# Feed-forward weight terms in six parts: three per head added by accumulating DMAs, three by GpSimd

## What is computed

```
xn = _layernorm(x)
x  = x + attention(xn) + ffn(xn)
attention: q,k,v = split(xn @ qkv_w + qkv_b); 16 heads of 128
           scores = q @ k.T + alibi (causal); softmax; ctx = attn @ v; ctx @ out_w + out_b
ffn:       gate = xn @ lut[gate_idx].T;  up = xn @ lut[up_idx].T
           h = silu(gate) * up;          out = h @ lut[down_idx].T
lut: 16 values; gate_idx, up_idx: 688x256; down_idx: 256x688
```

## Time and profile before

| | |
|---|---|
| median of 3 runs | 542.9 us (542.81 to 543.8) |
| the profiled execution | 543.26 us |
| its span in the trace | 541.5 us |
| busy | PE 493.8 us, DVE 414.2 us, POOL 403.6 us, ACT 360.9 us |

### The profile page before, as it was taken

The page is one execution under the profiler, slowest core; times in us unless marked ns, Lnnn a source line. Parts: engine busy times, 40 slices in busy tenths (PEclk is TensorE's granted clock), DMA queues, the critical chain, the costliest instruction groups (busy, mean ns, idle before and its releaser), DMA issues.

```text
span 541.5 us, 9700 instructions
## 1 busy us (share of the span) xinstructions
PE 493.8 (91%) x2826; PEld 422.4 (78%) x2826; DVE 414.2 (76%) x1067; ACT 360.9 (67%) x657; POOL 403.6 (75%) x312
## 2 busy tenths in 40 slices
PE   7896797999889988998899989997999989789998
PEld 6785576898779876987689768986798779578897
DVE  6796988788888878888788987888788886543541
ACT  3575867687767867595959685877678766824430
POOL 5533989788978998798969897889789979921400
PEclk9997999999999999999999999999999999979999
DMA  8204243332514070606160524134331514000001
GB/s 285 87 0 101 62 98 103 73 91 53 146 44 116 13 186 4 156 0 161 38 144 16 119 80 113 47 79 120 70 90 43 119 38 104 0 1 2 0 21 58
DMA packets 18948, 41.65 MB, mean 77 GB/s; under 512 B 4848, under 2 KB 7024, under 8 KB 18800
## 3 DMA queue, kind: packets, MB, share of 16 engines
q1 hardware_dynamic: 18928, 41.40, 30.2%
HBM read 11.83 MB, written 1.05 MB: 24 GB/s over the span
## 4 chain that ended last, share of the span: by engine, by line
POOL 44%; PE 23%; issue 21%; DVE 7%; ACT 3%; DMA 1%; POOLq 0%; DVEq 0%; ACTq 0%
POOL p_t_lo L1125 17%; POOL w_ffn L1153 15%; POOL work L1118 5%; PE ps_u L447 5%; PE ps_u L449 4%; PE ps_u L448 4%; DVE term L958 3%; PE ps_s L447 2%; PE ps_s L448 2%; PE ps_s L449 2%; POOL v_w_lo L1102 2%; POOL pad L1117 2%; POOL qk_w_lo L1097 2%; ACT ctx_t_hi L721 1%; DVE ctx_t_lo L898 1%
## 5 line engine op out<-in xcount | busy, mean ns | idle before, releaser
L1153 POOL TENSOR_TENSOR w_ffn<-w_ffn,term 128x1088 f32<-128x1088 f32 x60 | 155.0, 2584 | 45.4 <-DVE term L958 45.4
L1125 POOL TENSOR_TENSOR p_t_lo<-p_t_lo,p_t_hi 128x1024 fp32r<-128x1024 f32 (+2 forms) x60 | 133.1, 2251 | 0.0
L738 ACT ACTIVATE work<-work,neg_max 128x128 f32<-128x128 f32 (+7 forms) x128 | 99.0, 773 | 24.1 <-DVE neg_max L937 22.1
L937 DVE CUSTOM_DVE_ANT_0 work<-ps_s,alibi 128x128 f32<-128x128 f32 (+7 forms) x128 | 95.8, 749 | 0.0
L447 PE MATMUL ps_u<-p_t_hi,v_hi 128*128 128x512 f32 x192 | 70.5, 367 | 17.7 <-POOL p_t_lo L1125 17.4
L975 DVE STREAM_TRANSPOSE blocks<-work 128x512 f32<-128x512 f32 x120 | 65.3, 582 | 11.6 <-ACT work L750 11.6
L447 PE MATMUL ps_s<-k_hi,q_hi 128*128 128x256 f32 (+2 forms) x192 | 67.3, 350 | 5.3 <-DVE neg_max L937 5.3
L958 DVE TENSOR_SCALAR term<-codes,entry,table 128x1088 f32<-128x1088 uint8 x60 | 65.8, 1096 | 4.3 <-POOL w_ffn L1153 4.3
L449 PE MATMUL ps_u<-p_t_hi,v_lo 128*128 128x512 f32 x192 | 67.2, 350 | 0.0
L448 PE MATMUL ps_u<-p_t_lo,v_hi 128*128 128x512 f32 x192 | 67.0, 349 | 0.0
L448 PE MATMUL ps_s<-k_lo,q_hi 128*128 128x256 f32 (+2 forms) x192 | 65.8, 343 | 0.0
(11 more groups left out here) (148 smaller groups left out, 1271.1 us busy)
## 6 DMA issues: line engine op xcount, KB each, us to landing
p_t_lo<-blocks SPq DMA_DIRECT2D x240, 116.0 KB, 2.3
qk_raw<-w_qk SPq DMA_DIRECT2D x16, 256.0 KB, 2.7
w_ffn<-idx SPq DMA_DIRECT2D x1, 2176.0 KB, 11.0
v_raw<-w_v SPq DMA_DIRECT2D x8, 256.0 KB, 3.5
o_raw<-w_o SPq DMA_DIRECT2D x8, 256.0 KB, 2.9
out<-acc SPq DMA_DIRECT2D x8, 128.0 KB, 1.7
acc<-x SPq DMA_DIRECT2D x2, 256.0 KB, 3.0
acc<-x SPq DMA_DIRECT2D x1, 512.0 KB, 5.0
```

The lines of the kernel that those rows point to most:

```text
L738: act.activation(slot(i), slot(i), ACT.Exp, bias=neg_max[:, col:col + 1], scale=-1.0, accum_out=row_sum[:, col:col + 1]).then_inc(exp_done, 1)
L937: dve.tensor_tensor_reduce(slot(i).rearrange("p (b c) -> p b c", b=banks), made_of, alibi[:, p, S - width:S].rearrange("p (b c) -> p b c", ...
L1125: pool.tensor_tensor(rows, rows.bitcast(F32), chunk_rows(0, chunk).bitcast(F32), ALU.subtract).then_inc(upper_lo, 1)
L1153: pool.tensor_tensor(piece, piece, term[:, :], ALU.add).then_inc(term_added, 1)
```

## The change

`w_ffn` is now worked on in 6 parts (five of 726 columns and one of 722), and `term` has two buffers ("rooms"), used in turn. DVE does 6 look-ups per head in place of 4, at other steps. Parts 0, 1 and 2 are added to `w_ffn` by a DMA that POOL issues with `accum_op=ALU.add`, from `term` (SBUF) onto `w_ffn` (SBUF); ahead of each stands a 128x1 operation on POOL that carries the wait for the look-up. Parts 3, 4 and 5 are added by POOL as before. A look-up of part k now waits until part k - 2 has been added, by the DMA's semaphore or by POOL's. `stats`, `moments` and `ln` of the layernorm move into the buffer `alibi`, which makes room. In the last head the split of the first four weight pieces moves from steps 3 to 6 to steps 5 to 7.

```
-TERM_AT = (1, 3, 5, 7)
-SUM_AT = (1, 3, 6, 7)
+TERM_AT = {1: 0, 3: 1, 4: 2, 6: 3, NT: 4, 7: 5}
+ADD_AT = {1: 0, 3: 1, 5: 3, 6: 4, 7: 5}
+ROOMS = 2
+BY_DMA = 3
...
-TERMS = 4
-LUT_PIECE = WF // TERMS
+TERMS = 6
+LUT_PIECE = -(-WF // TERMS)
+SUMS = TERMS - BY_DMA
...
-        term = sb("term", [P, LUT_PIECE])
+        term = sb("term", [P, ROOMS * LUT_PIECE])
...
+        def wait_added(engine, before, part):
+
+            if part >= BY_DMA:
+                engine.wait_ge(term_summed, before * SUMS + (part - BY_DMA + 1))
+            else:
+                per = len(range(part % ROOMS, BY_DMA, ROOMS))
+                engine.wait_ge(term_added[part % ROOMS], before * (16 * per) + 16 * (part // ROOMS + 1))
...
-                        if 3 <= i < 7 and kind == LAST and p == 1:
-                            ffn_w_hi_of(i - 3)
+                        if i >= 5 and kind == LAST and p == 1:
+                            for piece in ((0,), (1,), (2, 3))[i - 5]:
+                                ffn_w_hi_of(piece)
...
-                    dve.wait_ge(term_added, n * (2 * TERMS) + (p - 1) * TERMS + part)
...
+                    heads = n * 2 + (p - 1)
+                    if part < ROOMS:
+                        wait_added(dve, heads - 1, part - ROOMS + TERMS)
+                    else:
+                        wait_added(dve, heads, part - ROOMS)
+                target = w_ffn[:, part_of(part)] if kind == FIRST and p == 0 else room_of_term(part)
+                dve.tensor_scalar(target, codes[:, part_of(part)], column(entry, n, p), column(table, n, p),
                                   ALU.is_equal, ALU.mult).then_inc(term_ready, 1)
...
                             invert(n, p, i)
+                            look_up(n, kind, p, TERM_AT[NT])
                             if upper:
                                 turn_blocks(n, p, QT + 2)
...
+            def add_term(n, p, part):
+
+                pool.wait_ge(term_ready, n * (2 * TERMS) + p * TERMS + part + 1)
+                if part >= BY_DMA:
+                    values = w_ffn[:, part_of(part)]
+                    pool.tensor_tensor(values, values, room_of_term(part), ALU.add).then_inc(term_summed, 1)
+                    return
+                col = 4 * NT + 1 + part
+                pool.tensor_tensor(pad[:, col:col + 1], entry[:, 0:1], entry[:, 0:1], ALU.add)
+                pool.dma_start(w_ffn[:, part_of(part)], room_of_term(part),
+                               accum_op=ALU.add).then_inc(term_added[part % ROOMS], 16)
...
                                 upper_lo_of(n, p, chunk)
+                                if chunk == 0:
+                                    add_term(n, p, 2)
+                        if i in ADD_AT and not (kind == FIRST and p == 0):
+                            add_term(n, p, ADD_AT[i])
...
-                            piece = w_ffn[:, part * LUT_PIECE:(part + 1) * LUT_PIECE]
-                            pool.tensor_tensor(piece, piece, term[:, :], ALU.add).then_inc(term_added, 1)
```

More of the change, by code:

```diff
@@ L235, in block_ffn @@
         based = sem("based")
-        iota_done, made, normed, term_added = sem("iota_done"), sem("made"), sem("normed"), sem("term_added")
+        iota_done, made, normed = sem("iota_done"), sem("made"), sem("normed")
+        term_added = [sem(f"term_{room}_added") for room in range(ROOMS)]
+        term_summed = sem("term_summed")
         qk_w_lo, v_w_lo, o_w_lo, ffn_w_lo = sem("qk_w_lo"), sem("v_w_lo"), sem("o_w_lo"), sem("ffn_w_lo")
@@ L370, in h_raw, with part_of, room_of_term, wait_last_terms @@
             return alibi[:, 0, (u % 2) * HALF:(u % 2 + 1) * HALF]
+        def part_of(part):
+            return slice(part * LUT_PIECE, min((part + 1) * LUT_PIECE, WF))
+        def room_of_term(part):
+            at = (part % ROOMS) * LUT_PIECE
+            return term[:, at:at + part_of(part).stop - part_of(part).start]
+        def wait_added(engine, before, part):
[4 more added lines that the diff above has]
+                engine.wait_ge(term_added[part % ROOMS], before * (16 * per) + 16 * (part // ROOMS + 1))
+        def wait_last_terms(engine, reached):
+            for part in range(max(reached - ROOMS, 0), reached):
+                wait_added(engine, HEADS - 2, part)
+            if reached > BY_DMA:
+                for part in range(BY_DMA):
+                    wait_added(engine, HEADS - 2, part)
         def all_pairs(engine, pair):
@@ L704, in _ @@
             act.wait_ge(made, 1)
-            act.activation(pad[:, 4 * NT:], eps[:, :], ACT.Sqrt)
+            act.activation(pad[:, 4 * NT:4 * NT + 1], eps[:, :], ACT.Sqrt)
             root(0)
@@ L810, in silu_of @@
                 if u < 2:
[L811 removed]
+                    wait_last_terms(act, TERMS)
                 else:
@@ L948, in look_up @@
                     dve.wait_ge(made, 6)
-                    dve.tensor_copy(codes[:, piece], w_ffn[:, piece].bitcast(I32)).then_inc(codes_ready, 1)
+                    dve.tensor_copy(codes[:, part_of(part)], w_ffn[:, part_of(part)].bitcast(I32)
+                                    ).then_inc(codes_ready, 1)
                     dve.wait_ge(codes_ready, part + 1)
-                elif kind == FIRST and part == 0:
-                    dve.wait_ge(based, NT)
-                else:
-                    dve.wait_ge(term_added, n * (2 * TERMS) + (p - 1) * TERMS + part)
[L955 to L958, removed]
+                    dve.wait_ge(small_landed, 32)
+                elif kind == FIRST and part < ROOMS:
+                    if part == 0:
+                        dve.wait_ge(based, NT)
+                else:
+                    heads = n * 2 + (p - 1)
[5 more added lines that the diff above has]
+                dve.tensor_scalar(target, codes[:, part_of(part)], column(entry, n, p), column(table, n, p),
                                   ALU.is_equal, ALU.mult).then_inc(term_ready, 1)
```

28 lines of the change are left out of this document (12 added, 16 removed).

## The result

The changed kernel takes **632.2 us** (median of 4 runs, 630.4 to 636.0) against 543.35 before (542.8 to 544.8) on the same chip. The ratio is 1.164, with a 95% interval of 1.158 to 1.170. It is 89 us slower, and the forecast was 536.

The account below looks back on a forecast made before the run. PE sets the pace in head A and waits in head B, 27.8 us in all for POOL. Heads B 8 x 0.8 = 6.4, heads A 0, last head 0.6: 7.0 us off 543.26, said as 536.0; range 524 to 552.

Parts of the forecast that it names:

- six short ones take as long as four: DVE's look-ups per head: six of the smaller parts cost the same total time as four before.
- is a third shorter: Long look-up beside POOL's chunks moves to step 4 and shrinks by a third; 0.4 us of the second chunk returns.
- rival 2: Accumulating DMA holds up SP's moves in head B, second of a pair: 542.3 us or 551 us; chance 0.14.
- 1 us later: Last move in head B lands this late: first half about -0.6 us, head B gains nothing, 542.3 us.
- 2 us later: Last move in head B lands this late: 8 x -1.0 us, 551 us, slower.
- rival 4: DVE waits for a DMA before a look-up: step 4 stalls 1.3 us in 15 heads, 556 us; chance 0.05.
- c: Length of one DMA issue on POOL, taken as 0.9 us, between 0.34 and 2.55.
- rival 1: DMA issues on POOL are dear: slower from c = 1.4 us, 548 us at 1.7, 560 at 2.55; chance 0.22.
- The forecast of -7: Whole kernel: 7.0 us gained, 6.4 from eight heads B, 0 from heads A, 0.6 from the last head.
- Head A: First head of a pair, PE full: 0.94 - c stays above 0, so neither loss nor gain.
- Last head: PE's wait for DVE behind a 2.34 us look-up shrinks: 0.6 us gained, between 0 and 2.
- The rule that I weighed: POOL's DMA issues: DVE's two-port mode blocks descriptor writing, so c grows by up to the look-up or mask-table instruction beside it.

Follow-up runs that it names:

- no_dma: The changed kernel with all six parts added by POOL at the same places and no DMA; 557.0 us (ratio 1.021).
- part2_aligned: The changed kernel with only part 2 added by a DMA, a 128x1 POOL operation and a wait behind its issue; 550.2 us (ratio 1.014).
- parts12_aligned: part2_aligned with part 1 also added by a DMA, operation and wait behind each issue, part 0 by POOL; 557.3 us (ratio 1.022).
- after_aligned: The changed kernel with a 128x1 POOL operation and a wait for it behind each DMA issue; 591.1 us (ratio 1.086).
- plain_dma: The changed kernel with a head's three DMAs as plain copies, so those parts hold only the last term; 602.8 us (ratio 1.108).
- late_qk_tiny: late_qk with each accumulating DMA cut to 16 of its 726 columns, the rest not added; 549.8 us (ratio 1.012).
- late_qk_nodma: late_qk with all six parts added by POOL, no DMA; 558.3 us (ratio 1.027).
- late_lookup: The changed kernel with part 3's look-up moved from step 6 to step 7, part 4's to the end of step 7; 568.8 us (ratio 1.044).
- late_qk: late_lookup with POOL's q/k weight split ahead of its adds of parts 3, 4 and 5, together in step 7; 561.1 us (ratio 1.031).
- parts01_dma: The changed kernel with only parts 0 and 1 added by DMAs, part 2 by POOL between the chunks; 598.3 us (ratio 1.097).
- before_step6: The kernel before with part 2's look-up at the end of step 6 in place of step 5, no DMA, four parts; 561.1 us (ratio 1.034).

## Why the prediction was wrong

The 89 us, step by step, from these runs (medians; steps of under 8 us are at the edge of the intervals, and another order of the steps could share the time out otherwise):

| kernel | us | step |
|---|---|---|
| before | 543.9 | |
| no_dma: six parts, two buffers, look-ups at other steps | 557.0 | +13 |
| part2_aligned: part 2 by a DMA | 550.2 | -7 |
| parts12_aligned: part 1 too | 557.3 | +7 |
| after_aligned: part 0 too | 591.1 | +34 |
| after: the wait behind the issues gone | 632.2 | +41 |

**The step that failed** is "six short ones take as long as four", with "is a third shorter". The look-ups take 106.7 us, not 65.8, and 91.4 in no_dma, without any issue. I followed the long look-up of before out of step 5 into step 4 and costed that. I did not ask what the new one in step 6 stands beside: POOL's last three chunks. The row to ask it of was there: 1.88 us beside a chunk, twice its length. I used it to lengthen a chunk by 0.4 us and not as a price for DVE. Shown is that the shut-out costs 41 to 48 us, that an issue ahead of the chunks causes it, and that a small operation with a wait behind the issue mends it. That POOL's parts run apart is an inference; no row shows its parts, and plain_dma speaks against it. The Trainium skill bears on it in two places. Perfetto Trace Analysis (DMA Instruction — SWDGE (GPSIMD)) has two of POOL's processors make the descriptors. SBUF — State Buffer (SBUF: two separate sides) has whichever of DVE and GpSimd starts first hold their shared ports for its whole instruction, while the other waits. By the second alone DVE would get in when the chunk that it met ends, as in no_dma; the 4.25 us of the changed kernel don't follow from it.

**The moves** (rival 2, 0.14) were the right mechanism and the wrong size. I bounded the term by "1 us later" and "2 us later"; ACT waited 4.2 us on average, eight times, 33.4 us. The traffic costs 34 to 41 us, and nearly all of it comes when part 0 goes by a DMA as well (parts12_aligned to after_aligned). In head B the DMAs of parts 0 and 1 land 5.4 and 6.2 us after their issues, and for 0.9 us both are in flight beside the moves. No row of before showed an accumulating transfer beside the moves. I had summed the landing at "4.7 us", and 4.3 was the median; but I asked of it only whether the buffer is free in time, which it is (no look-up waits for a DMA there, so rival 4 didn't come), and not what it does to the transfers beside it.

**The issue**, my largest doubt, was cheap: c = 0.62 us, under the 0.9 taken and far under the 1.4 of rival 1. The gain that I drew from it is real where nothing else breaks: -7 us for one issue (part2_aligned against no_dma), -8.5 for three (late_qk_tiny against late_qk_nodma). The forecast of -7 was thus of the right size for POOL's share, but all these kernels are slower than the kernel before, and the agreement is of a sum over one engine with pairs of kernels that it wasn't made for.

**Head A** "no loss": +4 us, from the same look-up (3.15 us there). **Last head** "0.6 us gained": PE waits 6.9 us for DVE where it waited 4.2.

**The rule that I weighed**, that DVE's two-port mode holds up an issue, showed in few rows and cost little. In the changed kernel an issue's row lasts 0.86 to 1.03 us. Six issues in late_lookup, late_qk, late_qk_tiny and parts01_dma last 1.53 to 1.55 us, each beside DVE's mask-table operation (`alibi`, 1.21 us in place of the usual 0.68). The dear direction was the other one: POOL's chunks held up DVE's look-up.

**PE's clock.** Head B's granted clock of 0.82 is a mean. By windows of the changed kernel (length, busy us per engine, granted clock, DMA share, GB/s) it is at the upper of its two levels (2.4 GHz) from 290 to 300 us, ahead of the waits, and at the lower one (1.2 GHz) behind the waits of 4.69 us (until 304.32) and 3.74 us (until 317.43):

```profile
290.00:300.00 10.00, 9.63 (x62) 8.58 (x60) 6.93 (x20) 3.79 (x10) 5.58 (x10) 1.00 0.99 199
...
304.00:306.00 2.00, 1.68 (x4) 1.39 (x5) 2.00 (x7) 2.00 (x4) 2.00 (x4) 0.50 0.12 23
318.00:322.20 4.20, 4.20 (x19) 3.91 (x18) 2.34 (x4) 0.60 (x1) 0.00 (x0) 0.50 0.49 111
```

A 128x512 matmul right behind the first wait took 0.79 us, against 0.50, and PE is 30.6 us busier for the same matmuls. Over its whole run part2_aligned, with most of the long waits gone, has a clock of 0.991, the changed kernel 0.905. I take the clock as a follower of the waits that makes them dearer; it wasn't tested apart.

**What stays open.** The 13 us of no_dma aren't placed in full: PE waits 27.7 us for chunks, 10.3 more than before, and 7.9 less for norms. before_step6 says that a look-up in step 6 is dear in itself, but late_qk_nodma, with none there, is no faster than no_dma (558.3 against 557.0; POOL's adds stand otherwise in it too). A kernel with part 0 alone by a DMA wasn't tried, so its 34 us aren't told apart from those of two transfers at once. And what an issue does to the chunks behind it is known only by its effect and its cure.

## What to carry to other kernels

Work moved off the bounding engine changes what the others stand beside. For each instruction that moves, list its new neighbours on the engines with which it shares ports, and price it by the worst row of that pairing, not by its length alone. A DMA has three prices: its issue, its landing, and what it does to the transfers in flight; when one of those has under 1 us of slack, as the moves had here, expect to pay for another beside it. And where an issue on GpSimd is followed by long operations back to back with DVE working beside them, try a small operation with a wait behind the issue.

## What the hardware showed that I had not expected

- An accumulating DMA's issue on GpSimd takes 0.62 us of its time (0.87 us in its row), for 128 rows of 726 or of 16 columns alike, and a copy's takes the same 0.62 us (0.60 in its row). But the chunks after it kept a DVE look-up out for 4.3 us, where without an issue it took 2.3; a 128x1 operation and a wait (0.7 us) restored that, and took 598.5 us to 550.5.
- An accumulating DMA, SBUF to SBUF, 363 KB: 4.3 us to landing, against 3.1 for a copy, with twice the DMA engine time (15.5% of 628.6 us against 7.5% of 599.8 for 16.73 MB). The copy costs the kernel 4 us over DMAs of 16 columns, the accumulating one 34.
- Beside it SP's issues got longer: 16 moves in 11.66 us in place of 10.05.
